# Row tiles 0 to 4 of an attention and feed-forward kernel in a written-out order

## The chip, the cores and the metric

The kernel runs on one core of one Trainium2 chip. The metric is device microseconds (us) of one launch. The kernel before takes 547.33 us, the median of 3 runs (546.87 to 547.88). TensorE (PE) multiplies, VectorE (DVE), ScalarE (ACT) and GpSimd (POOL) work on vectors, and SyncE (SP) issues nearly all DMA transfers.

## The reference

For eight batches of 512 rows of 512 numbers the kernel computes a cross attention against a context of 77 rows per batch, adds it to its input, and then a feed-forward layer with fake-quantised activations and weights, which is added too:

```python
q = layernorm(x) @ Wq                    # 8 heads of 64
k, v = context @ Wk, context @ Wv        # context: 8 x 77 x 384
attn = softmax(q @ k.T / 8)
x = x + (attn @ v) @ Wo + bo
xq = fake_quant(layernorm(x), clip_x)    # one scale for the whole tensor
h = silu(xq @ quant(w_gate).T) * (xq @ quant(w_up).T)     # 1408 wide
x = x + fake_quant(h, clip_down) @ quant(w_down).T
```

The two scales of `fake_quant` need the maximum over all rows, so the kernel has three stages: attention (about 20 to 300 us of the span), the gate and up products (to about 430 us), the down product. The change lies in the first.

## The kernel before

**Tiling.** The 4096 rows are 32 row tiles of 128 rows, n = 0 to 31; a batch b is four of them, and t = n % 4 is the place of a tile in its batch. Products that need full accuracy are made of three float32r products each, of high and low halves: the high half is an ACT copy (`split_hi`, `qo_hi`, `PT_high`), the low half a DVE or POOL subtraction (`split_lo`, `qo_lo`, `PT_low`).

**The steps of a row tile**, in the kernel's names:
- `q_chunk(b, m)`: 12 matmuls make a quarter of the queries of a batch in a QO bank; ACT copies it to `qs`. It needs all eight halves of the transposed input, `xTs`. `q(b,m)` for short.
- `S(n)`: 4 matmuls of scores into SP. `soft_max` and `soft_sub` (DVE) read SP and so free it for S(n+1). `soft_exp` (ACT), `soft_sum` and `soft_rec` (DVE), `soft_norm` (POOL, two instructions into `PN`) follow.
- `PT(n)`: 5 transposes into PTP; `PT_high` (ACT) and `PT_low` (DVE) take it to `pts`.
- `PV_rest(b)` and `PV(b, j)`, once a batch: attention times values, 24 matmuls into four banks; `qo_hi` (ACT) and `qo_lo` (DVE) take each to `os`. The values come back from DRAM by `load_vb(b)`, 12 small DMAs into `vbd`.
- `wo(n)`: 12 matmuls, then `residual` (DVE) adds the input with the bias, which `first_bias(n)` (POOL) had added. `first_stats`, `second_stats` and the like are the layer norms.
- `v_rows(r)`, r = 0 to 4: 9 matmuls make 128 rows of values for all batches; ACT and DVE halve them in `vst` (two slots), and SP stores them.
- Beside this, the feed-forward weights are turned to integers, 26 tiles i: `w_load` (SP), `w_top`, `w_scale`, `w_inverse` (DVE), `w_round` (ACT), `w_integer` (POOL and a store on SP). 22 of the tiles are 512 wide, and 4, rows of `w_down`, 1408 wide; `W_ORDER` says which is which.

**What sets the order.** There is no scheduler. Each call of `add` or `dma` appends an instruction to the queue of its engine, with semaphore waits; each engine runs its queue strictly in that order. So the order of the calls in the text is the order on every engine, SP's DMA queue among them. `attend(s)` is the written schedule of one step: it holds the weight tile s-1, the scores of tile s+1, the transposes of tile s, the output product of tile s-5, and so on, at places that depend on t. The steps 0 to 3 had exceptions of their own inside `attend` (`if s == 2` and the like), and `v_rows(0)` to `v_rows(4)` stood in between.

Of the kernel before, what the change touches and what calls it, by code (L numbers as in the profile page):

```python
# [62 lines left out]
def block_kernel(nc, x, xT, ctxT, Wq, Wk, Wv, Wo, bo, clip_x, clip_h, w_gate, w_up, w_down, out):  # L63
# [3 lines left out]
    NT, NI = 32, 11  # L67
# [6 lines left out]
    with ctx:  # L74
# [461 lines left out]
        def PV_rest(b):  # L536

            banks = []
            for j in range(2):
                at = state["use"] % 2  # L540
                state["use"] += 1
                banks.append((at, state["banks"][at], state["free"][at]))
            for k in range(2):
                banks.append((None, SP[:, 512 * k:512 * k + 512], (t_sub[min(4 * b + 4, NT - 1)],)))
            pv_at[b] = banks

            def fn(e):
                for i, (hv, hp) in enumerate(((0, 0), (0, 1), (1, 0))):
                    for j in range(4):
                        q = slice(32 * j, 32 * j + 32)  # L550
                        m = e.matmul(banks[j][1], vbd[q, hv, 4, :], pts[q, hp, 4, :], start=(i == 0), stop=False)
                return m
            add("pe", fn, [t_pl[4 * b + 3], t_vb[b], *(t for bank in banks for t in bank[2])], "qo_mm")

        def PV(b, j):
# [12 lines left out]
            if j < 2:  # L568
                state["free"][at] = (t_oss[b, j],)
# [86 lines left out]
        for at, tile in ((4, 22), (8, 23), (12, 24), (16, 25)):  # L656
            W_ORDER.insert(at, tile)
# [59 lines left out]
        t_pz = add("pool", lambda e: e.memset(PN[:, :, 512:640], 0.0), [t_ctxl, t_wkl], "c_pz")  # L717
        for k in range(4):
            split_hi(1, k)
            split_lo(1, k, ("dve", "pool")[k % 2])  # L720
        v_rows(0)
        S(0)
        soft_max(0)
        soft_sub(0)
        soft_exp(0)
        soft_sum(0)
        soft_rec(0)
        soft_norm(0)
        v_rows(1)
        S(1)  # L730
        soft_max(1)
        soft_sub(1)
        v_rows(2)
        soft_exp(1)
        for n in range(4, XR):
            load_xn(n, [])
        t_sge = add("act", lambda e: e.activation(sge[:, :], clips[:, :], ACT.Exp, scale=-1.0),
                    [t_clip], "sg_e")
        t_sg = add("dve", lambda e: e.tensor_scalar_add(sgp[:, :], sge[:, :], 1.0), [t_sge], "sg_p")
        t_sg = add("dve", lambda e: e.reciprocal(sg[:, :], sgp[:, :]), [t_sg], "sg")  # L740

        DEFER = (1, 2)

        def attend(s):
# [3 lines left out]
                  "pv": t == 0 and b >= 1}  # L748
# [14 lines left out]
            if s < 26 and s != 2:  # L763
# [3 lines left out]
            late_low = s - 1 >= 0 and (s - 1) % 4 in DEFER  # L767
            if t == 0:
# [33 lines left out]
            elif t < 3:  # L802
                if t == 1 and b + 1 < NB and s != 1:
                    q_chunk(b + 1, t)
# [12 lines left out]
                if b + 1 < NB:  # L817
                    if t == 2 or s == 1:
                        q_chunk(b + 1, t)
                    if t == 2:  # L820
                        q_chunk(b + 1, 3)
                if s == 2:
                    PT(s)
                    split_hi(2, 0)
                    split_hi(2, 1)
                    PT_high(s)
                    split_hi(2, 2)
                    split_hi(2, 3)
                    first_stats(5)
                    first_aggr(5)  # L830
                    PT_low(s)
                    split_lo(2, 2, "dve")
                    split_lo(2, 3, "dve")
# [17 lines left out]
            else:  # L851
                when("s", S, s + 1)
                when("s", soft_max, s + 1)
                if s > 3:
                    PT_low(s - 1)
                else:
                    v_rows(4)
                    PT(s)
                    PT_high(s)
# [12 lines left out]
                if s == 3:  # L872
                    q_chunk(2, 0)
# [14 lines left out]
            if s == 0:  # L888
                v_rows(3)
            if s == 1:  # L890
                for n in range(3):
                    first_bias(n)
# [534 lines left out]
```

How the kernel before makes its waits and increments, by code:

```python
    def run(self, engine, e):  # L47
        for need, fn, sem, by in self.queue[engine]:
            for s, v in need:
                e.wait_ge(s, v)
            ins = fn(e)
            if sem is not None:
                ins.then_inc(sem, by)
```

## Time and profile before

| | us |
|---|---|
| median of 3 runs | 547.33 |
| the profiled execution | 547.3 |
| its span | 545.5 |
| PE busy in the span | 528.1 (97%) |
| DVE busy | 475.3 (87%) |
| ACT busy | 294.2 (54%) |
| POOL busy | 231.8 (42%) |

The granted clock of PE is full throughout. Of the chain of work that ended last, PE holds 73% and DVE 12%. Matmuls are pipelined: one of 512 columns is shown 0.39 us long, and the next starts 0.23 us after it. So lengths of work on PE are best read from start to start.

### The profile page before, as it was taken

What the parts mean: (1) busy time and instruction counts of PE and PEld (TensorE: products, weight loads), DVE (VectorE), ACT (ScalarE), POOL (GpSimd) and SP (SyncE); (2) the same over time, 40 slices, a digit from 0 to 9 for tenths busy, and PEclk for the clock granted to TensorE, in tenths of its full rate; (3) what the DMA queues carried; (4) which work ended last, traced back from release to release, by engine and by line L of the source; (5) the groups of instructions that cost most, each with busy time, mean ns of one, the idle gap of its engine ahead of it and who ended that gap; (6) DMA issues with size and microseconds to landing.
All of it is one profiled execution on the core that took longest, in us unless ns stands there. A gap on an engine that the chain in (4) does not pass through costs nothing.

```text
span 545.5 us, 8102 instructions
## 1 busy us (share of the span) xinstructions
PE 528.1 (97%) x2740; PEld 355.9 (65%) x2740; DVE 475.3 (87%) x879; ACT 294.2 (54%) x414; POOL 231.8 (42%) x349
## 2 busy tenths in 40 slices
PE   8989889999999999999999899999999999999997
PEld 7868678787888878888788644444444445544444
DVE  4966988999989899898989799999999988899884
ACT  4834645556465654554534646555545533999500
POOL 4385858769596895856553000000000000055442
PEclk9999999999999999999999999999999999999999
DMA  8809375765668465545949955850442220399987
GB/s 315 275 41 301 92 210 171 226 215 160 214 212 272 143 216 178 178 129 165 203 88 313 282 122 242 283 141 22 116 117 44 72 38 5 123 328 234 159 106 127
DMA packets 82943, 93.83 MB, mean 172 GB/s; under 512 B 47085, under 2 KB 50157, under 8 KB 82645
## 3 DMA queue, kind: packets, MB, share of 16 engines
q1 hardware_dynamic: 77877, 84.13, 49.9%
q0 software_dynamic: 4320, 7.87, 9.6%
q10 hardware_dynamic: 704, 1.31, 0.7%
q8 instruction: 22, 0.36, 0.3%
q14 instruction: 20, 0.16, 0.1%
HBM read 47.51 MB, written 37.78 MB: 156 GB/s over the span
## 4 chain that ended last, share of the span: by engine, by line
PE 73%; DVE 12%; SPq 6%; DMA 3%; issue 2%; ACT 1%; POOL 1%; ACTq 0%; DVEq 0%; POOLq 0%
PE SP L1137 13%; PE QO L1137 13%; PE QO L192 5%; PE QO L194 4%; PE QO L193 4%; SPq L37 4%; PE SP L463 4%; PE QO L1294 4%; PE PTP L1294 3%; PE SP L1294 3%; SPq L41 2%; PE MI L583 2%; PE MI L582 2%; PE MI L581 2%; PE WOP L1294 2%
## 5 line engine op out<-in xcount | busy, mean ns | idle before, releaser
L45 POOL DMA_DIRECT2D out<-n2b x30 | 30.3, 1045 | 207.4 <-DVE n2b L1327 207.4
L1144 ACT ACTIVATE sil<-QO,fsc 128x512 f32<-128x512 f32 x87 | 59.8, 687 | 70.9 <-PE QO L1137 69.3
L1137 PE MATMUL SP<-nT,wgu 128*128 128x512 bf16 x340 | 87.3, 379 | 0.4
L1137 PE MATMUL QO<-nT,wgu 128*128 128x512 bf16 x340 | 87.3, 379 | 0.1
L1148 DVE SCALAR_TENSOR_TENSOR h<-SP,fsc,sil 128x512 f32<-128x512 f32 x87 | 65.1, 748 | 8.7 <-PE SP L1137 7.1
L504 POOL TENSOR_TENSOR PN<-P,rs 128x512 f32<-128x512 f32 x64 | 44.3, 714 | 50.2 <-DVE rs L496 50.2
L1151 DVE TENSOR_REDUCE hmx<-h 128x1 f32<-128x512 f32 x87 | 59.7, 686 | 3.0
L487 ACT ACTIVATE P<-P,r 128x616 f32<-128x616 f32 x32 | 26.0, 812 | 63.7 <-DVE P L483 63.7
L1137 PEld LDWEIGHTS SP<-nT,wgu 128*128 128x128 bf16 x340 | 32.9, 98 | 41.4 <-DVE h L1148 2.5
L1137 PEld LDWEIGHTS QO<-nT,wgu 128*128 128x128 bf16 x340 | 33.2, 98 | 40.2 <-ACT sil L1144 0.3
L192 PE MATMUL QO<-xTs,wqs 128*128 128x512 f32 x124 | 50.4, 407 | 2.3 <-DVE xTs L223 2.0
L1261 ACT ACTIVATE h<-h,magic,g 128x1536 f32<-128x1536 f32 (+2 forms) x38 | 47.8, 1350 | 3.3 <-DVE g L1073 3.3
L194 PE MATMUL QO<-xTs,wqs 128*128 128x512 f32 x124 | 48.5, 391 | 0.0
L193 PE MATMUL QO<-xTs,wqs 128*128 128x512 f32 x124 | 48.3, 390 | 0.0
L463 PE MATMUL SP<-kst,qs 128*128 128x154 f32 x248 | 38.1, 296 | 4.0 <-DVE P L483 1.8
L602 POOL TENSOR_TENSOR xn<-xn,bob 128x512 f32<-128x512 f32 x32 | 41.3, 1294 | 0.0
L686 ACT ACTIVATE wraw<-wraw,magic,wiv 128x512 f32<-128x512 f32 (+1 forms) x26 | 24.1, 928 | 31.2 <-DVE wiv L679 31.2
L463 PEld LDWEIGHTS SP<-kst,qs 128*128 128x128 f32 x248 | 34.5, 190 | 5.9 <-DVE P L483 2.2
L631 ACT ACTIVATE n<-x,mr,r 128x512 f32<-128x512 f32 x31 | 25.0, 808 | 15.5 <-POOL mr L625 15.5
L1264 DVE TENSOR_SCALAR wgu<-h 128x1536 bf16<-128x1536 f32 (+2 forms) x39 | 29.3, 757 | 1.2 <-ACT h L1261 0.7
L192 PEld LDWEIGHTS QO<-xTs,wqs 128*128 128x128 f32 x124 | 23.3, 188 | 7.8 <-issue 2.2
L493 DVE TENSOR_REDUCE sm<-P 128x8 f32<-128x616 f32 x32 | 25.1, 785 | 2.6 <-ACT P L487 1.7
(224 smaller groups left out, 1203.3 us busy)
## 6 DMA issues: line engine op xcount, KB each, us to landing
xTr<-in_xT SPq DMA_DIRECT2D x8, 1024.0 KB, 7.9
xn<-in_x SPq DMA_DIRECT2D x32, 256.0 KB, 3.8
out<-x SPq DMA_DIRECT2D x32, 256.0 KB, 2.9
n_rows<-n SPq DMA_DIRECT2D x32, 256.0 KB, 2.7
n2b<-n_rows SPq DMA_DIRECT2D x32, 256.0 KB, 3.8
out<-n2b POOLq DMA_DIRECT2D x30, 256.0 KB, 6.5
h_spill<-h SPq DMA_DIRECT2D x2, 2816.0 KB, 9.3
h<-h_spill SPq DMA_DIRECT2D x6, 768.0 KB, 7.2
```

The costliest lines, as they stand in the source:

```text
L192: e.matmul(ps, lh, rh, start=(i == 0), stop=False)
L193: e.matmul(ps, lh, rl, start=False, stop=False)
L194: m = e.matmul(ps, ll, rh, start=False, stop=(i == n - 1))
L463: m = e.matmul(o, qs[:, b % 2, j, w], kst[:, b, j, :], start=(j % 2 == 0), stop=True, skip_group_check=True)
L504: t_norm[n] = add("pool", lambda e, to=to, rb=rb, l0=l0, l1=l1: e.tensor_tensor(to, u[:, :, l0:l1], rb, ALU.mult), [t_rec[n], t_PT.get(n - ...
L602: t_xb[n] = add("pool", lambda e: e.tensor_tensor(xn[:, n % XR, :], xn[:, n % XR, :], bob[:, :], ALU.add), [t_bn1[n], t_bo], "xb")
L1137: m = e.matmul(ps, wv_[:, k, col:col + 128], nT[:, b % 2, :, k, :], start=(k == 0), stop=(k == 3))
L1144: t_sil[n] = add("act", lambda e: e.activation(sil[:, n % SR, :], gp, ACT.Silu, scale=fsc[:, ic:ic + 1]), [t_g[n], t_fs, t_h.get(n - SR)], ...
L1148: t_h[n] = add("dve", lambda e: e.scalar_tensor_tensor(out=hv, in0=up, scalar=fsc[:, 11 + ic:12 + ic], in1=sil[:, n % SR, :], op0=ALU.mult ...
L1151: t_hm[n] = add("dve", lambda e: e.tensor_reduce(hmx[:, n:n + 1], hv, AX.X, ALU.max, apply_absolute_value=True), [t_h[n]], "hmx")
L1261: a = add("act", lambda e: e.activation(hv, hv, ACT.Identity, bias=magic[:, :], scale=g2[:, 1, 1:2]), [t_g2] + ([t_back[b, p]] if b < 2 el ...
L1294: mm = e.matmul(ps, hq[:, i % 2, k, tt * 128:tt * 128 + 128], wd[:, k, :], start=(k == 0), stop=(k == NI - 1))
```

## The change

It touches the order alone; every instruction that computes is still there.

- Row tiles 0 to 4 are no longer made by `attend(0)` to `attend(3)` but by a list of calls ahead of the loop, and the loop begins with `attend(4)`. At that point the same steps have been done as before, and in addition `PV_rest(0)` and `PV(0, 0..3)`, which stood in `attend(4)`.
- `v_rows` is cut in two: `v_mm(r)` (the matmuls) and `v_out(r)` (the halves and the store). S(0) comes directly behind q(0,3), and the value rows come behind scores.
- `PV_rest(0)` uses the banks MI and WOP for its pairs 0 and 1 and QO for 2 and 3, in place of QO and SP; so S(5) waits for no copy of it.
- The loads of `xn` and of weight tiles 0 and 1 stand ahead of the stores of the value rows.
- The wide tiles move from the places 4, 8, 12, 16 of `W_ORDER` to 9, 13, 17, 21. A tile at place i is converted in step i+1: so from steps with t = 1 to steps with t = 2.

```diff
-        def v_rows(r):
+        def v_mm(r):
...
+            v_at[r] = qo_bank(pairs, 512, m, [t_wvl, t_ctxl])
+
+        def v_out(r):
...
+            th = add("act", lambda e: e.activation(hi, bank, ACT.Copy), [t, t_v.get(r - 2)], "qo_hi")
...
+            t_v[r] = dma("sp", vd[r * 128:r * 128 + m], vst[0:m, r % 2], [th, tl], f"st_v{r % 2}")
...
-            if t == 1 and b > 0:
+            if t == 1 and b > 1:
                 free += [t_oss[b - 1, 2], t_oss[b - 1, 3]]
...
-            banks = []
+            banks = [] if b else [(None, MI[:, :], ()), (None, WOP[:, :], (t_c,))]
...
-        for at, tile in ((4, 22), (8, 23), (12, 24), (16, 25)):
+        for at, tile in ((9, 22), (13, 23), (17, 24), (21, 25)):
...
+        S(0)
+        v_mm(0)
+        soft(0, "max", "sub", "exp")
+        v_out(0)
+        v_mm(1)
+        S(1)
+        soft(0, "sum", "rec", "norm")
+        soft(1, "max", "sub")
+        v_out(1)
+        load_vb(0)
+        v_mm(2)
+        soft(1, "exp")
+        S(2)
+        split_lo(1, 0, "dve")
+        soft(1, "sum", "rec", "norm")
+        first_bias(0)
+        soft(2, "max", "sub")
+        v_out(2)
+        split_lo(1, 2, "dve")
+        t_xT[2] = load_xT(2, t_xTs[1])
+        v_mm(3)
+        soft(2, "exp")
+        PT(0)
+        PT_high(0)
+        v_out(3)
+        q_chunk(1, 0)
...
+        q_chunk(1, 3)
...
+        S(4)
+        soft(4, "max", "sub")
+        PV_rest(0)
+        PV(0, 2)
+        soft(4, "exp")
+        split_hi(2, 3)
+        split_lo(2, 2, "dve")
+        PV(0, 3)
+        soft(4, "sum", "rec", "norm")
+        split_lo(2, 3, "dve")
+        PV(0, 0)
+        PV(0, 1)
+        q_chunk(2, 0)
+        first_bias(4)
+        w_tops(2)
+        w_round(2)
+        w_integer(2)
...
-        for s in range(28):
+        for s in range(4, 28):
             attend(s)
```

**DVE, between the scores of tile 4 and the query chunk q(2,0).** `xTs` is a low half of the input of batch 2, `mx`, `P`, `sm`, `rs` are the softmax, `pts` is `PT_low`, `vst` the last value rows. Before:

```order
L223 TENSOR_TENSOR pts<-PTP,pts 128x5x128
L223 TENSOR_TENSOR xTs<-xTr,xTs 128x512 x2
L476 TENSOR_REDUCE mx<-SP 128x8
L211 TENSOR_TENSOR vst<-QO,vst 104x512
L483 TENSOR_TENSOR P<-SP,mx 128x616
```

Now, where `os` is the low half of a pair of attention times values:

```order
L486 TENSOR_REDUCE mx<-SP 128x8
L493 TENSOR_TENSOR P<-SP,mx 128x616
L577 TENSOR_TENSOR os<-QO,os 128x512
L223 TENSOR_TENSOR xTs<-xTr,xTs 128x512
L577 TENSOR_TENSOR os<-QO,os 128x512
L503 TENSOR_REDUCE sm<-P 128x8
L506 RECIPROCAL rs<-sm 128x8
L223 TENSOR_TENSOR xTs<-xTr,xTs 128x512
L577 TENSOR_TENSOR os<-MI,os 128x512
L577 TENSOR_TENSOR os<-WOP,os 128x512
```

The two low halves that q(2,0) waits for stood ahead of the scores of tile 4; now the second stands behind two `os` halves and the sum of tile 4.

**ACT, at the same place.** `qs` is the copy of a query chunk, `wraw` is `w_round`. Before, the chunk is q(2,0), and the rounding is that of weight tiles 2 and 3:

```order
L219 ACTIVATE qs<-QO 128x512
L686 ACTIVATE wraw<-wraw,magic,wiv 128x512 x2
L565 ACTIVATE os<-SP 128x512 x2
L565 ACTIVATE os<-QO 128x512 x2
L219 ACTIVATE pts<-PTP 128x5x128
```

Now (the first `qs` after the `os` copies is q(2,0)):

```order
L576 ACTIVATE os<-QO 128x512
L497 ACTIVATE P<-P,r 128x616
L219 ACTIVATE xTs<-xTr 128x512
L576 ACTIVATE os<-QO 128x512
L576 ACTIVATE os<-MI 128x512
L576 ACTIVATE os<-WOP 128x512
L219 ACTIVATE qs<-QO 128x512
L697 ACTIVATE wraw<-wraw,magic,wiv 128x512 x2
```

The rounding of weight tiles 2 and 3 stood ahead of the four `os` copies and now stands behind them and behind the chunk q(2,0), which comes after all of PV(0).

**SP, the DMA queue, from the second load of transposed input on.** `v_halves` are stores of value rows, `vbd` the 12 loads of `load_vb(0)`. Before:

```order
L37 DMA xTr<-in_xT 128x4x512
L37 DMA v_halves<-vst 128x1024 x3
L37 DMA xn<-in_x 128x512 x5
L37 DMA wraw<-in_ffn_w_gate 128x512
L37 DMA xTr<-in_xT 128x4x512
L37 DMA v_halves<-vst 128x1024
L37 DMA wraw<-in_ffn_w_gate 128x512
L37 DMA wgu_ints<-wint 128x512
L37 DMA wraw<-in_ffn_w_gate 128x512
L37 DMA vbd<-v_halves 64x4x64 x4
L37 DMA vbd<-v_halves 13x2x64 x8
```

Now:

```order
L37 DMA xTr<-in_xT 128x4x512
L37 DMA xn<-in_x 128x512 x5
L37 DMA wraw<-in_ffn_w_gate 128x512 x2
L37 DMA v_halves<-vst 128x1024 x2
L37 DMA vbd<-v_halves 64x4x64 x4
L37 DMA vbd<-v_halves 13x2x64 x8
L37 DMA v_halves<-vst 128x1024
L37 DMA xTr<-in_xT 128x4x512
L37 DMA v_halves<-vst 128x1024
```

Loads went ahead of the stores, and `load_vb(0)` ahead of the third store of value rows. For batch 1 the row of SP is the same as before: store of weight tile 2, load of tile 4, `xTr`, 12 `vbd`, store of tile 3, load of tile 5.

## Rows read from the trace of the kernel before

**Rows 1.** Busy time of each engine in two stretches; count of instructions in brackets.

```profile
core 0: us, PE busy (x) PEld busy (x) DVE busy (x) ACT busy (x) POOL busy (x), PEclk, DMA share, GB/s
30.30:73.60 43.30, 37.34 (x195) 29.84 (x193) 33.18 (x60) 21.86 (x38) 32.14 (x37) 1.00 0.53 165
...
96.30:300.00 203.70, 202.30 (x1078) 167.45 (x1079) 186.73 (x373) 109.08 (x167) 139.13 (x238) 1.00 0.64 195
```

**Rows 2.** What PE waited for, 30 to 80 us: total, times, longest.

```profile
PE SP L463 <- DVE P L483: 1.8, 1, 1.8
PE SP L463 <- DVE os L566: 1.6, 1, 1.6
PE QO L192 <- DVE xTs L223: 1.1, 1, 1.1
PE QO L551 <- DMA vbd<-v_halves: 0.9, 1, 0.9
PE SP L463 <- ACT qs L219: 0.6, 1, 0.6
```

**Rows 3.** Timeline of PE: start us, length us, instruction, [idle before].

```profile
30.33 0.39 PE L192 MATMUL QO<-wvs,cts 128*128 128x512 f32 x1
...
46.37 1.21 PE L463 MATMUL SP<-kst,qs 128*128 128x154 f32 x8
47.31 0.49 PE L192 MATMUL QO<-xTs,wqs 128*128 128x512 f32 x1
...
50.18 0.71 PE L516 MATMUL PTP<-identF,PN 128*128 128x128 f32 x5
50.73 1.22 PE L463 MATMUL SP<-kst,qs 128*128 128x154 f32 x8
...
67.61 0.50 PE L551 MATMUL QO<-pts,vbd 32*128 32x512 f32 x2 [0.90 <-DMA vbd<-v_halves]
...
68.51 0.50 PE L559 MATMUL SP<-pts,vbd 128*128 128x512 f32 x1
...
71.38 0.71 PE L516 MATMUL PTP<-identF,PN 128*128 128x128 f32 x5
73.64 1.29 PE L463 MATMUL SP<-kst,qs 128*128 128x154 f32 x8 [1.55 <-DVE os L566]
...
96.29 0.47 PE L192 MATMUL QO<-xTs,wqs 128*128 128x512 f32 x1
```

**Rows 4.** Timeline of POOL and DVE, 31.5 to 34 us.

```profile
29.47 4.61 POOL L223 TENSOR_TENSOR wos<-wor,wos 128x2048 fp32r<-128x2048 f32 x1
...
31.68 2.95 DVE L223 TENSOR_TENSOR xTs<-xTr,xTs 128x512 fp32r<-128x512 f32 x1 [3.35 <-ACT xTs L219]
```

**Rows 5.** The chain that ended last, 30 to 38 us: start, us, what.

```profile
34.55 0.68 DVE xTs L223
```

**Rows 6.** Timeline of ACT and DVE, three instructions.

```profile
30.53 0.60 ACT L219 ACTIVATE qs<-QO 128x512 f32<-128x512 f32 x1 [2.12 <-PE QO L194]
...
47.62 0.80 DVE L476 TENSOR_REDUCE mx<-SP 128x8 f32<-128x616 f32 x1 [1.76 <-PE SP L463]
48.45 0.80 DVE L483 TENSOR_TENSOR P<-SP,mx 128x616 f32<-128x616 f32 x1
```

**Rows 7.** Stores of value rows: time from issue to landing.

```profile
DMA to landing us min/median/max: 2.6/5.8/9.0
```

**Rows 8.** Timeline of SP, 69 to 83 us.

```profile
70.06 0.37 SPq L37 DMA_DIRECT2D wgu_ints<-wint  x1
...
71.62 9.82 SPq L37 DMA_DIRECT2D vbd<-v_halves  x12
...
82.04 0.42 SPq L37 DMA_DIRECT2D wraw<-in_ffn_w_gate  x1
```

**Rows 9.** DMA issues, 60 to 120 us: count, KB each, median us to landing.

```profile
wraw<-in_ffn_w_gate SPq DMA_DIRECT2D x6, 256.0 KB, 2.9
```

**Rows 10.** Timeline of DVE and ACT in step 6.

```profile
86.97 0.67 DVE L670 TENSOR_REDUCE wmx<-wraw 128x1 f32<-128x512 f32 x1
...
91.87 0.69 ACT L219 ACTIVATE pts<-PTP 128x640 fp32r<-128x640 f32 x1
```

More of the change, by code:

```diff
@@ L542, in PV_rest @@
                 banks.append((at, state["banks"][at], state["free"][at]))
-            for k in range(2):
-                banks.append((None, SP[:, 512 * k:512 * k + 512], (t_sub[min(4 * b + 4, NT - 1)],)))
+            if b:
+                for k in range(2):
+                    banks.append((None, SP[:, 512 * k:512 * k + 512], (t_sub[min(4 * b + 4, NT - 1)],)))
             pv_at[b] = banks
@@ L567, in PV @@
                               [th, *waits], "qo_lo")
-            if j < 2:
+            if at is not None:
                 state["free"][at] = (t_oss[b, j],)
@@ L717, in block_kernel, with soft, row_stats, w_tops @@
         t_pz = add("pool", lambda e: e.memset(PN[:, :, 512:640], 0.0), [t_ctxl, t_wkl], "c_pz")
+        def soft(n, *steps):
+            for step in steps:
+                {"max": soft_max, "sub": soft_sub, "exp": soft_exp, "sum": soft_sum, "rec": soft_rec,
+                 "norm": soft_norm}[step](n)
+        def row_stats(n):
+            first_stats(n)
+            first_aggr(n)
+            first_scale(n)
+        def w_tops(i):
+            w_top(i)
+            w_scale(i)
+            w_inverse(i)
         for k in range(4):
             split_hi(1, k)
[L720 to L734, printed above, removed]
+        split_lo(1, 1)
+        split_lo(1, 3)
         for n in range(4, XR):
             load_xn(n, [])
+        w_load(0)
+        w_load(1)
+        S(0)
[24 more added lines that the diff above has]
+        q_chunk(1, 0)
+        soft(2, "sum", "rec", "norm")
+        first_bias(1)
+        PT_low(0)
+        S(3)
+        row_stats(3)
+        soft(3, "max", "sub")
+        PT(1)
+        PT_high(1)
+        soft(3, "exp")
+        q_chunk(1, 1)
+        PT_low(1)
+        soft(3, "sum", "rec", "norm")
+        first_bias(2)
+        first_bias(3)
         t_sge = add("act", lambda e: e.activation(sge[:, :], clips[:, :], ACT.Exp, scale=-1.0),
@@ L740, in block_kernel @@
         t_sg = add("dve", lambda e: e.reciprocal(sg[:, :], sgp[:, :]), [t_sg], "sg")
+        w_tops(0)
+        v_mm(4)
+        w_round(0)
+        w_integer(0)
+        v_out(4)
+        t_flat = [t_v[4], t_v[3], t_wol, ("qo_mm", c.count["qo_mm"])]
+        PT(2)
+        PT_high(2)
+        w_load(2)
+        q_chunk(1, 2)
+        PT_low(2)
+        row_stats(4)
+        PT(3)
+        PT_high(3)
+        w_tops(1)
+        w_round(1)
+        w_integer(1)
+        w_load(3)
+        q_chunk(1, 3)
+        PT_low(3)
+        row_stats(5)
+        for k in range(3):
+            split_hi(2, k)
+        split_lo(2, 0)
+        split_lo(2, 1)
+        S(4)
[15 more added lines that the diff above has]
+        w_integer(2)
+        row_stats(6)
+        first_bias(5)
+        first_bias(6)
         DEFER = (1, 2)
@@ L761, in turned @@
                 PT_high(s)
-            if s < 26 and s != 2:
+            if s < 26:
                 w_load(s)
@@ L802, in attend @@
             elif t < 3:
[L803 removed]
+                if t == 1 and b + 1 < NB:
                     q_chunk(b + 1, t)
@@ L816, in attend @@
                 when("w", w_inverse, s - 1)
[L817 to L833, printed above, removed]
+                if b + 1 < NB and t == 2:
+                    q_chunk(b + 1, 2)
+                    q_chunk(b + 1, 3)
                 when("w", w_round, s - 1)
@@ L853, in attend @@
                 when("s", soft_max, s + 1)
[L854 to L859, printed above, removed]
+                PT_low(s - 1)
                 when("s", soft_sub, s + 1)
-                if s == 3:
-                    PT_low(s)
                 when("s", soft_exp, s + 1)
-                if s > 3 and b + 2 < NB:
+                if b + 2 < NB:
                     split_lo(b + 2, 3, "dve")
@@ L887, in attend @@
                 when("n2", normed, s - 6)
[L888 to L892, printed above, removed]
             when("s", soft_norm, s + 1)
@@ L895, in attend @@
             if more:
-                for k in range(2 if s == 2 else 3):
+                for k in range(3):
                     split_lo(b + 2, k)
```

58 lines of the change are left out of this document (22 added, 36 removed).

## The prediction, made before the changed kernel ran

> **What bounds the kernel now.** I read first the busy time by stretch. From 96 us to the end of attention PE is busy 202.30 of 203.70 us [rows 1]: there PE sets the pace, and the change moves no matmul of that stretch. From 30.3 to 73.6 us PE is busy 37.34 of 43.30 us, so 6.0 us are idle [rows 1]. The list of PE's waits names all of them: S(1) behind a late subtraction (1.8), S(5) behind a copy of PV(0) (1.6), q(2,0) behind a low half (1.1), PV_rest(0) behind the last `vbd` load (0.9), S(4) behind its query copy (0.6) [rows 2]. The timeline then gives lengths from start to start: S 0.94 us (46.37 to 47.31), a query chunk behind it 2.87 (to 50.18), PT 0.55 (to 50.73), PV_rest 0.90 (67.61 to 68.51), PV 2.87 (to 71.38) [rows 3]. A block of values is 9 matmuls of 0.23, 2.1 us, and 0.1 more behind scores.
>
> The change removes no work. It is worth what it takes from the 6.0 us, less what it puts in their place, and less what is lost again before 96.29 us, the start of q(3,0) [rows 3]. From there on the order is the old one but for the wide tiles. So I replay the new order by hand from 30.33 us, where q(0,3) has been issued.
>
> **Part 1: tiles 0 to 4, step by step.**
>
> (a) S(0) directly behind q(0,3). It waits for the query copy, which runs 30.53 to 31.13 [rows 6]; before, value rows started at 30.33 and hid it [rows 3]. S(0) starts at 31.16: 0.8 us of new idle.
>
> (b) S(0), values 0 and 1, S(1), values 2, S(2), values 3: 3 x 0.94 + 4 x 2.1 + 3 x 0.1 = 11.5, to 42.7. Do the scores wait? A max starts 1.25 us behind its scores, the subtraction 0.83 later, and takes 0.80 [rows 3, 6]: 2.9 us in all. For S(0) that is 34.1, and S(1) is due at 36.4; for S(1) 39.3, and S(2) is due at 39.6. No wait; the 1.8 us of rows 2 goes. It had come from DVE standing in a low half of `xTs` for 2.95 us [rows 4], whose own length is 0.68 [rows 5]; that op is now behind the scores.
>
> (c) PT(0) to 43.3, then q(1,0), which waits for the low half (1,2). DVE has ahead of it the low half of value rows 1, half (1,0), sum and reciprocal of tile 1, max and subtraction of tile 2 (to 43.05) and value rows 2 (to 43.6). Alone the half would end at 44.3. But `first_bias(0)` stands on POOL from 42.9 to 44.2, and in rows 4 the same DVE op, started at 31.68 beside a POOL op that ended at 34.08, ended only at 34.63, 0.55 us behind it. So I let it end 0.55 behind the bias, at 44.7, and q(1,0) start at 44.8: 1.5 us idle. Bounds: 1.0 if the two don't meet; 2.1 if the DVE op also meets the next POOL op.
>
> The Trainium skill, page "SBUF — State Buffer", section "SBUF: two separate sides", says that VectorE with two SBUF inputs and GpSimd hold a port pair in turn, each for its whole instruction. By that rule, the trace agrees (34.08 and 34.63); a sum without it would come out 0.4 us lower.
>
> (d) q(1,0), S(3), PT(1), q(1,1), values 4, PT(2), q(1,2), PT(3), q(1,3): 4 x 2.85 + 0.94 + 3 x 0.55 + 2.1 = 16.1, to 60.9. Softmaxes, PT_low and the halves of value rows are done 0.3 us or more ahead of each.
>
> (e) S(4) directly behind q(1,3) waits for its query copy: 0.8 us (0.6 before, rows 2). S(4) at 61.7.
>
> (f) S(4), PV_rest(0), PV(0): 1.05 + 0.90 + 2.87, to 66.55, without a wait, since `vbd` is issued 40.4 to 50 now. The 0.9 goes. Then q(2,0) waits for low half (2,3), which now stands behind PV's copies. The subtraction of tile 4 ends at 61.7 + 3.0 = 64.7. ACT: `os` high of pair 2 to 65.25, exp (0.7 from start to start) to 65.95, `split_hi(2,3)` to 66.5, `os` high of pair 3 to 67.05. DVE: `os` low 0.6, sum 0.83, reciprocal 0.12, half (2,3) 0.68: 69.3. q(2,0) starts at T = 69.3: 2.8 us idle where 1.1 stood. This is the largest new wait. Bounds 2.0 to 3.7: pair 2 and exp overlap less or more by one op of 0.8.
>
> (g) q(2,0) 2.8, PT(4) 0.55: S(5) at T + 3.35 = 72.65, with no wait for PV's copies. Before it was 73.64 [rows 3]. So here the kernel is 1.0 us ahead.
>
> **Part 2: what is given back.** w_round(2) stands on ACT behind the copy of q(2,0). That copy ends at T + 3.6, the rounding at T + 4.5, `w_integer(2)` on POOL (0.6) at T + 5.1. SP is in order: store of tile 2, load 4, `xTr`, then 12 `vbd` issues of 9.82 us together, store of tile 3, load of tile 5. From that store to load 5 SP took 70.06 to 82.04, 12.0 us [rows 8]. So load 5 is issued at T + 17.1 = 86.4, and lands 2.9 later [rows 9]: L = 89.3. Queued behind it on DVE is all that follows `w_top(5)`, which before ran at 86.97 [rows 10] and 1 us ahead would be due at 86.0. DVE had 2.3 us of slack at its next wait for PE; the rest is late. Sum 7, the scale, w_round(5), four `split_hi` and PT_high(6) follow one another: from `w_top(5)` to the end of PT_high(6) rows 10 show 5.6 us, of which 0.4 was a wait for exp, so 5.2. Then PT_low(6) 0.8, subtraction 0.7, low half (3,3) 0.7 and 0.1: q(3,0) at L + 7.6 = 96.9. Before it was at 96.29 [rows 3]. The 1.0 us gained has become 0.6 us lost. Bounds of this part: nothing given back (load in time), or 1.3 more if the load takes 4.2 us behind the `vbd` packets.
>
> **Part 3: wide tiles at t = 2.** DVE has 1.0 us more in steps 10, 14, 18, 22 and 1.0 less in the step before. Both lie ahead of the same DVE wait for the output product, so that DVE arrives there at the same time. ACT and POOL get 0.7 more each, ahead of `split_hi` and behind the low halves. I take 0; bounds -0.5 to +1.0, a quarter of a us for each of the four.
>
> **Part 4: the rest.** `PV_rest(0)` in other banks, the split of `v_rows` and the clip constants cost nothing on PE; the same number of matmuls is issued. The early loads of `xn` and of tiles 0 and 1 take away two DVE waits that PE did not share.
>
> **Sum.** Against the profiled execution, 547.3 us (span 545.5): + 0.6 = 547.9. The median of the runs, 547.33, differs from it by less than 0.1 us, so the sum stands for both. As (c) and (f) may as well be shorter by half an op, I put 547.8.
>
> **Rivals.**
> 1. *The gain stays (load 5 hidden).* If SP's issues run faster or w_round(2) is sooner, L is at 86 or less, and the 1.0 us of (g) goes to the end: 546.3; with (f) at its low bound 545.5. For it: PE is full from 96 us on, so nothing else takes it. Against it: L must come 3 us sooner, and the 12.0 us of SP repeat the same DMAs. Chance 0.26.
> 2. *The old waits simply go.* S(0), q(1,0), S(4) and q(2,0) find their inputs ready and 5 of the 6 us are won: 542 to 544. Against it: steps (a) and (e) are waits for a copy behind its own matmuls, and no order hides them here. Chance 0.05.
> 3. *The store of value rows holds ACT.* `v_out(4)` waits on ACT for the store of value rows 2, because they share a slot of `vst`, and that store is now behind the 12 `vbd` issues: issued at 50.0. ACT needs it at 55.1; behind `v_out(4)` are PT_high(2), the copy of q(1,2) and PT_high(3), and PT(3) on PE waits for PT_low(2). Landings were 2.6 to 9.0 us [rows 7]. It decides from a landing of 5.1 us; at the median 5.8 it costs under 1, at 9.0 it costs 3.5: then T is later by as much: 548.5 to 551.3. Against it: the 9.0 was behind 2 MB of other loads, and now nearly nothing is ahead. Chance 0.12.
> 4. *Low half (2,3) later still, or wide tiles costly*: the upper bounds of (f) or part 3, 548.5 to 549.5. Chance 0.17.
> 5. Forecast: 547.8, own range 547.0 to 548.5. Chance 0.40.
>
> A difference of 0.2% is 1.1 us, about what a measurement tells from no change: 546.2 and 548.4 are the limits. Rival 2 and most of rival 1 are faster, with a little of the forecast's lower side: 0.29. Rivals 3 and 4 and a little of the forecast are slower: 0.30. The rest, 0.41, is the same. The range is 545.7 to 549.6: below it lie rival 2 and the extreme of rival 1, above it the long landings of rival 3.
>
> **What would show it.** In the profile of the changed kernel: the wait of S(1) gone; S(0) waiting 0.7 to 0.8 for `qs`; q(1,0) waiting 1 to 2 for `xTs`; PE idle 2.0 to 3.7 us ahead of q(2,0), waiting for DVE `xTs`; S(5) near 72.7; DVE `w_top` (wmx) waiting near 86 us about 3 us for the DMA of `wraw`; q(3,0) near 96.9. The prediction is wrong if DVE doesn't wait for that load, if ACT waits for a store ahead of a `vst` copy, or if PE shows new idle time after 100 us.

## The result, and the profile of the changed kernel

The changed kernel takes 560.31 us, the median of 3 runs (559.49 to 563.32), against 547.33: a ratio of 1.0249, with a 95% interval of 1.0214 to 1.0284. It is 13 us slower, and the time forecast, 547.8 with a range up to 549.6, was wrong.

The profiled execution took 563.32 us (span 561.5). The busy times in the two stretches, as in [rows 1]:

```profile
30.30:73.60 43.30, 37.70 (x188) 30.26 (x188) 31.82 (x58) 20.00 (x34) 26.90 (x30) 0.96 0.39 121
96.30:300.00 203.70, 190.80 (x1008) 155.87 (x1007) 176.06 (x350) 102.55 (x154) 136.98 (x226) 0.99 0.59 178
```

The part that was replayed step by step shows about the same busy time, at a mean granted clock of 0.96, so with a little less work in it. Most of the loss is in the other stretch, where PE was busy 202.30 us and is now busy 190.80. The profiled execution is the slowest of the three; 2.0 us of its loss lie ahead of q(3,0), the rest behind.

**Tiles 0 to 4.** PE's waits from 30 to 80 us, which answer to [rows 2]: total, times, longest.

```profile
PE QO L192 <- DVE xTs L223: 4.1, 2, 2.7
PE SP L473 <- ACT qs L219: 1.4, 2, 0.7
PE PTP L526 <- DVE pts L223: 0.2, 1, 0.2
```

The same on PE's timeline: S(0), q(1,0), S(4), q(2,0), its fifth matmul, S(5), and q(3,0), which answers to the last line of [rows 3].

```profile
31.10 1.32 PE L473 MATMUL SP<-kst,qs 128*128 128x154 f32 x8 [0.69 <-ACT qs L219]
44.84 0.47 PE L192 MATMUL QO<-xTs,wqs 128*128 128x512 f32 x1 [1.41 <-DVE xTs L223]
61.89 1.32 PE L473 MATMUL SP<-kst,qs 128*128 128x154 f32 x8 [0.69 <-ACT qs L219]
69.70 0.64 PE L192 MATMUL QO<-xTs,wqs 128*128 128x512 f32 x1 [2.66 <-DVE xTs L223]
71.43 0.63 PE L193 MATMUL QO<-xTs,wqs 128*128 128x512 f32 x1
74.67 1.22 PE L473 MATMUL SP<-kst,qs 128*128 128x154 f32 x8
98.32 0.47 PE L192 MATMUL QO<-xTs,wqs 128*128 128x512 f32 x1 [0.67 <-DVE xTs L223]
```

Steps (a) to (f) came within 0.4 us of the forecast. Behind the 2.66 us of idle the matmuls are 0.63 us long and 0.43 apart, where they were 0.39 and 0.23: the granted clock is 0.67 of full in 70 to 75 us, about 1.6 us lost. In the profile of the first experiment the same wait (2.63) has no such stretch behind it.

DVE's low half (1,2) beside POOL's bias addition, as in [rows 4]:

```profile
42.87 1.27 POOL L613 TENSOR_TENSOR xn<-xn,bob 128x512 f32<-128x512 f32 x1
43.48 1.21 DVE L223 TENSOR_TENSOR xTs<-xTr,xTs 128x512 fp32r<-128x512 f32 x1
```

POOL ends at 44.14 and DVE at 44.69, again 0.55 us behind.

**The load of weight tile 5** (step 6 takes it), as in [rows 8, 10]: the 12 `vbd` issues, the load behind them on SP, and `w_top(5)`.

```profile
77.75 9.33 SPq L37 DMA_DIRECT2D vbd<-v_halves  x12
...
87.68 0.42 SPq L37 DMA_DIRECT2D wraw<-in_ffn_w_gate  x1
```

```profile
90.74 0.69 DVE L681 TENSOR_REDUCE wmx<-wraw 128x1 f32<-128x512 f32 x1 [3.28 <-DMA wraw<-in_ffn_w_gate]
```

**The rest of the attention.** PE's waits from 80 to 315 us, then the longest of DVE's. Before, the same list for PE has 0.9 for `xTs` and 0.3 for `pts` in this stage.

```profile
PE PTP L526 <- DVE pts L223: 5.1, 4, 1.7
PE SP L473 <- DVE os L577: 4.2, 4, 1.2
PE QO L192 <- DVE xTs L223: 3.2, 5, 0.7
PE QO L562 <- DVE pts L223: 0.3, 1, 0.3
```

```profile
DVE pts L223 <- ACT pts L219: 6.6, 6, 1.6
DVE wmx L681 <- DMA wraw<-in_ffn_w_down: 6.5, 4, 2.2
DVE bn L599 <- DMA xn<-in_x: 5.3, 5, 1.6
```

That is 12.8 us on PE. One wait of each kind stands ahead of the first wide tile and belongs to the late tile 5 and the late row of SP behind it (0.36 ahead of PT(7), 0.67 ahead of q(3,0), 0.49 ahead of S(9)), and the last line is the same as before. The other 11.0 us follow the four wide tiles: 0.63 to 0.67 for `xTs` behind each of them, 1.3 to 1.75 for `pts` behind three (not the third), 1.2 for `os` behind three (not the first, where the clock had fallen). Read back from PE in batch 2, this is **chain 1**: load of the wide tile on SP, `w_top`, `w_round`, four `split_hi`, `PT_high(10)`, `PT_low(10)`, PT(11), q(4,0).

```profile
118.89 0.42 SPq L37 DMA_DIRECT2D wraw<-in_ffn_w_down  x1
```

```profile
124.77 1.62 DVE L681 TENSOR_REDUCE wmx<-wraw 128x1 f32<-128x1408 f32 x1 [2.17 <-DMA wraw<-in_ffn_w_down]
...
131.67 0.82 DVE L223 TENSOR_TENSOR pts<-PTP,pts 128x640 fp32r<-128x640 f32 x1 [1.56 <-ACT pts L219]
```

```profile
127.40 1.57 ACT L697 ACTIVATE wraw<-wraw,magic,wiv 128x1408 f32<-128x1408 f32 x1 [2.93 <-DVE wiv L690]
128.87 2.17 ACT L219 ACTIVATE xTs<-xTr 128x512 fp32r<-128x512 f32 x4
130.95 0.68 ACT L219 ACTIVATE pts<-PTP 128x640 fp32r<-128x640 f32 x1
```

```profile
132.64 0.74 PE L526 MATMUL PTP<-identF,PN 128*128 128x128 f32 x5 [1.75 <-DVE pts L223]
134.01 0.47 PE L192 MATMUL QO<-xTs,wqs 128*128 128x512 f32 x1 [0.63 <-DVE xTs L223]
```

The load was issued at 118.89, behind the 12 `vbd` issues and one store. In the kernel before, the wide load went 3.9 us ahead of them:

```profile
101.98 0.44 SPq L37 DMA_DIRECT2D wraw<-in_ffn_w_down  x1
...
105.88 9.66 SPq L37 DMA_DIRECT2D vbd<-v_halves  x12
```

DVE's first read takes 1.62 us (a tile 512 wide takes 0.67), ACT's rounding 1.57 (0.82).

**Chain 2** leads to the scores of the second tile of the next batch, behind batch 3 to S(17). It starts at the same `w_round`, for which the `split_hi` and so POOL's low halves wait. In batch 3 POOL has no gap from 166.10 to 178.38: three low halves, the wide integer op, the norms, the softmax, the next weight tile's integer op, and `mr` (row norm). ACT's `normed` waits for it, the rounding of the next tile and the `os` copies stand behind, and PE waits for DVE's `os`.

```profile
169.94 1.69 POOL L703 TENSOR_SCALAR wint<-wraw 128x1408 bf16<-128x1408 f32 x1
...
178.11 0.27 POOL L636 TENSOR_SCALAR mr<-mv,r 128x1 f32<-128x1 f32 x1
```

```profile
178.41 0.82 ACT L642 ACTIVATE n<-x,mr,r 128x512 f32<-128x512 f32 x1 [2.56 <-POOL mr L636]
179.13 0.80 ACT L697 ACTIVATE wraw<-wraw,magic,wiv 128x512 f32<-128x512 f32 x1
179.83 1.06 ACT L576 ACTIVATE os<-SP 128x512 fp32r<-128x512 f32 x2
```

```profile
181.88 1.29 PE L473 MATMUL SP<-kst,qs 128*128 128x154 f32 x8 [1.24 <-DVE os L577]
```

This run of POOL is not new. Before, it went without a gap from 156.51 to 168.09 us, 11.6 us in place of 12.3, and `normed` waited for its end too, but only 1.13 us, and PE did not wait:

```profile
168.12 0.82 ACT L631 ACTIVATE n<-x,mr,r 128x512 f32<-128x512 f32 x1 [1.13 <-POOL mr L625]
```

### The profile page after: what moved, and what is told of

Its sections match the earlier page's. It is cut to its first block, busy times and chain, and to the rows that moved or that the text cites. A ratio compares the mean times of both kernels' runs of the same rounds, so it can differ in the third digit from the quotient of the medians.

```text
span 561.5 us, 8093 instructions
## 1 busy us (share of the span) xinstructions
PE 532.4 (95%) x2733; PEld 357.4 (64%) x2740; DVE 474.0 (84%) x879; ACT 293.6 (52%) x414; POOL 231.3 (41%) x349
## 4 chain that ended last, share of the span: by engine, by line
PE 55%; DVE 11%; SPq 10%; POOL 8%; DMA 6%; issue 5%; ACT 3%; ACTq 0%; DVEq 0%; POOLq 0%
PE SP L1194 13%; PE QO L1194 12%; SPq L37 10%; DMA wraw<-in_ffn_w_down 4%; PE PTP L1351 3%; PE QO L1351 3%; PE SP L1351 3%; POOL xTs L223 3%; PE QO L192 2%; PE QO L193 2%; PE QO L194 2%; PE SP L473 2%; PE WOP L1351 2%; POOL wint L703 2%; DMA wkr<-in_xattn_Wk 1%
## 5 line engine op out<-in xcount | busy, mean ns | idle before, releaser
L192 PE MATMUL QO<-xTs,wqs 128*128 128x512 f32 x124 | 51.9, 418 | 7.3 <-DVE xTs L223 7.3
L193 PE MATMUL QO<-xTs,wqs 128*128 128x512 f32 x124 | 49.6, 400 | 0.0
L194 PE MATMUL QO<-xTs,wqs 128*128 128x512 f32 x124 | 49.6, 400 | 0.0
L486 DVE TENSOR_REDUCE mx<-SP 128x8 f32<-128x616 f32 x31 | 24.5, 789 | 10.6 <-PE SP L473 10.4
L223 DVE TENSOR_TENSOR pts<-PTP,pts 128x640 fp32r<-128x640 f32 x31 | 25.2, 813 | 6.1 <-ACT pts L219 6.1
```

Source lines behind the costliest of these rows:

```text
L192: e.matmul(ps, lh, rh, start=(i == 0), stop=False)
L193: e.matmul(ps, lh, rl, start=False, stop=False)
L194: m = e.matmul(ps, ll, rh, start=False, stop=(i == n - 1))
```

## The experiments

Each has 3 rounds; a ratio is to the kernel before on the same chip. "Waits" are PE's in the attention from 80 us on; the kernel before has 1.2. The runs f3 to f7 stand in their own parts below.

| | median us | ratio, 95% | waits |
|---|---|---|---|
| changed kernel | 560.31 | 1.0214 to 1.0284 | 12.8 |
| e1 wide tiles at the old places | 549.86 | 1.0026 to 1.0059 | 3.4 |
| e2 only the wide tiles moved | 558.44 | 1.0160 to 1.0229 | 10.6 |
| e3 old phase, one batch later | 549.85 | 1.0019 to 1.0053 | 3.1 |
| e4 wide tiles at t = 3 | 557.99 | 1.0153 to 1.0217 | 9.2 |
| f1 load cut | 558.36 | 1.0184 to 1.0230 | 9.0 |
| f2 conversion cut | 553.81 | 1.0093 to 1.0134 | 5.3 |
| g1 store later | 561.63 | 1.0212 to 1.0266 | 11.6 |
| g2 load cut, store later | 557.94 | 1.0141 to 1.0209 | 9.3 |
| h1 store later, norm behind `os` | 568.91 | 1.0351 to 1.0425 | 14.4 |
| h2 norm behind `os` | 567.19 | 1.0319 to 1.0410 | 14.0 |
| h3 load cut, store later, norm behind `os` | 558.37 | 1.0154 to 1.0234 | 8.5 |
| i1 store and norm later | 561.88 | 1.0233 to 1.0304 | 10.8 |
| i2 load cut, store and norm later | 553.74 | 1.0075 to 1.0147 | 5.7 |

### Is it the written-out part or the wide tiles?

```diff
 e1_old_places: the changed kernel with
+        for at, tile in ((4, 22), (8, 23), (12, 24), (16, 25)):
 e2_before_new_places: the kernel before with
+        for at, tile in ((9, 22), (13, 23), (17, 24), (21, 25)):
 e3_later_same_phase and e4_one_step_on: the changed kernel with
+        ((8, 22), (12, 23), (16, 24), (20, 25))
+        ((10, 22), (14, 23), (18, 24), (22, 25))
```

> The changed kernel, wide weight tiles back at places 4, 8, 12, 16. Theory P (the wide tile's load at places 9, 13, 17, 21 is issued on SP behind the 12 vbd loads and lands late, 11 of the 13 us): 547.5 to 549.5 us, no DVE wait for a w_down load, PE idle from 100 to 300 us about 1 us. Rival O (the written-out order of tiles 0 to 4 costs most of the 13 us): 556 to 560. The wait of DVE for weight tile 5 (3.3 us near 87 us in the changed kernel) stays under both.

> The kernel before, with nothing changed but the wide tiles at places 9, 13, 17, 21. Theory P: 556 to 559 us, and PE waits 1.2 to 1.8 us for pts and 0.6 for xTs once in each of four batches. Rival O: 547 to 548.5.

> The changed kernel, wide tiles at places 8, 12, 16, 20: four steps later than before, but loaded in a step with t = 0, ahead of the vbd loads. Theory P: same as with the old places within 1 us, 547.5 to 549.5. Rival L (later as such is what costs, as rows, stores and weights pile up): 553 to 560.

> The changed kernel, wide tiles at places 10, 14, 18, 22: loaded in a step with t = 2, not behind the vbd loads, converted in a step with t = 3. Theory P: 548 to 552, DVE waits under 0.5 us for a w_down load. Rival W (the length of the wide tile on DVE, ACT and POOL, 1.0, 0.75 and 0.75 us more, is what a step other than t = 1 can't hold, whenever it lands): 556 to 562, as at 9, 13, 17, 21 or worse.

The wide tiles cost 10.4 us in the new order (560.31 to 549.86) and 10.9 in the old one (558.44 to 547.59 in that call). So two things are left to explain: these 10.5 us, and the 2.3 us by which e1 is slower than before. That e3 equals e1 says that the phase in the batch decides, not which batch. At t = 3 there is no DVE wait for the load, yet the cost is 8.1 us, through another row:

```profile
PE QO L562 <- ACT qs L219: 6.2, 4, 1.6
```

Here the wide rounding stands on ACT ahead of the copy of q(b+2,0), and PV_rest waits for its bank. So length alone is enough to cost time, where it falls on a chain without slack. This is the rival's time (556 to 562); the theory that the late load is all had asked for 548 to 552.

### Load or length?

```diff
 f1_wide_load_cut: in w_load
+            n = 4 if i > 9 else n
 f2_wide_narrow_conv: in w_top, w_round and w_integer
+            v = wraw[:, i % 2, 0:(n if i < 10 else 4) * 128]
```

> The changed kernel (wide tiles at 9, 13, 17, 21); the last three of the four wide tiles load only 512 of their 1408 columns, and are still converted over all 1408. Left out: the other columns of the load. Theory P (late landing of the wide load): three of four losses of about 2.7 us shrink to under 0.7 us: 551 to 554 us. Rival W (the length of the conversion): 558 to 560.5, as the changed kernel.

> The changed kernel; the wide tiles are loaded in full, but the last three are converted (maximum, rounding, integers) over 512 columns only. Left out: the rest of their conversion. Theory P alone: 558 to 560. Rival W alone: 551 to 553. Both, one behind the other on the same chain (landing, maximum, rounding, split_hi, PT_high, PT_low): 554 to 557, as 1.0 us of DVE and 0.75 of ACT go in each of three batches.

For the three tiles that were cut, the length gives 6.5 us (f2: 553.81, just under the 554 to 557 expected if load and length both cost). The load gives 2.0: f1 is within the rival's times, and its interval overlaps that of the changed kernel, so this run alone doesn't tell the gain from nothing. f2 shortens the op on DVE, ACT and POOL at once; no run says which of the three counts most. In f1, PE's waits for `pts` and `xTs` fell to 1.0 and 2.3 us, but the one for `os` rose from 4.2 to 5.4. Chain 1 was relieved and chain 2 took over.

### What carries the wait for os?

My first theory for chain 2 was SP's order: its store of the wide tile waits for POOL and stands ahead of the load of `xn`, for which DVE waits 5.3 us.

```diff
 g1_store_behind_out, g2_cut_and_store_behind (with f1's cut): in step t = 3
-            if s < 26:
+            if s < 26 and not later:
                 w_load(s)
...
                 x_in()
+                if later:
+                    held.pop()()        # store of the wide tile
+                    w_load(s)
```

> The changed kernel, with SP's order altered around the wide tiles: the store of a wide tile and the load behind it, which both wait for POOL's long integer op, now stand behind the store of the rows x and the load of xn of the same step, not ahead of them. Nothing else is changed. Theory of two chains: the wait S(4b+1) <- DVE os (4.2 us in 4 in the changed kernel) comes only through this store (POOL integer late, SP held, xn load late, DVE bn late), so it goes, and the first chain (wide load late, DVE and ACT late, PT and q late, 8.3 us) stays: 555.0 to 557.5, with the DVE wait for xn near 1 us in all and PE's wait for os under 1. Rival (one chain: all lateness is that of the load and of the longer vector work, SP's order only changes its name): 559 to 561, the os wait is replaced by a longer wait of PT or q.

> The same order on SP, and the last three of the four wide tiles are loaded only 512 columns wide, though converted over all 1408 columns (the other 896 columns of these tiles hold old data, so the output of the down product is not that of the reference). With the load cut alone the kernel took 558.36, and its largest PE wait was os (5.4 us in 5). Theory of two chains: with both cut, what is left of the 10.5 us is the longer DVE and ACT work itself: 552.0 to 554.5; os wait under 1.5 us. Rival: the length of the conversion is all, 557 to 558.5.

That theory fell. DVE's wait for `xn` is gone in g1, and PE's wait for `os` is still 4.2 us in 4; g2 came to its rival's time. Batch 3 of g1 shows why:

```profile
177.24 0.82 ACT L642 ACTIVATE n<-x,mr,r 128x512 f32<-128x512 f32 x1 [2.59 <-POOL mr L636]
```

```profile
180.71 1.29 PE L473 MATMUL SP<-kst,qs 128*128 128x154 f32 x8 [1.25 <-DVE os L577]
```

From the wide integer op (168.74) to the scores it is 11.97 us, in the changed kernel 11.94 (169.94 to 181.88). By these rows the chain runs over POOL and ACT, and the wait for `xn` had stood beside it. So `normed`, which waits for POOL, was put behind the `os` copies.

```diff
 h1_norm_behind_os (g1 with it), h2_norm_behind_os_only, h3_all_three_cut (g2 with it): in t == 0
-                when("n2", normed, s - 6)
...
                         PV(b - 1, j)
+                when("n2", normed, s - 6)
```

> The kernel with the wide store behind the row store (561.63), and in the steps with t = 0 the norm of tile s-6 on ACT, which waits for POOL's mr, stands behind the four os copies and not ahead of them. POOL theory (POOL is busy without a gap from 164.9 to 177.2 us, wide integer among it; ACT's norm waits 2.6 us for its mr, and the os copies stand behind the norm): the wait S(4b+1) <- DVE os, 1.2 us in each of 4 batches, goes: 556.0 to 558.0, ACT's wait for mr ahead of os gone, PE's wait for os under 1.5 us in all. Rival (the os copies are late through w_round or PE itself): 560 to 562, os wait as before.

> The changed kernel with that move of the norm alone; SP's order is as in the changed kernel, so the load of xn stands behind the wide store, and DVE's statistics, the scale and w_round of the next weight tile wait for it (wiv ends at 178.64 us, mr at 178.38). If POOL's chain and SP's chain end together in front of the os copies, as these two ends say: 558.5 to 560.5, at most 0.4 us a batch gained, os wait 0.8 to 1.1 each. If POOL's alone decides and SP's is harmless: 555.5 to 557.5. If neither matters: 560 to 562.

> Load of the last three wide tiles cut to 512 columns (the rest of these tiles is old data, as before), the wide store behind the row store, and the norm behind the os copies; the conversion is at its full length. With the first two alone it was 557.94, with an os wait of 5.4 us in 5. POOL theory: 552.0 to 553.5, os wait under 1.5 us; what is left above 549.9 is the longer DVE and ACT work ahead of PT and q (xTs, pts waits 3 to 4 us) and the wait of the first wide tile, which is loaded in full. Rival: 556.5 to 558.

Measured were 568.91 us (ratio 1.0351 to 1.0425), 567.19 (1.0319 to 1.0410) and 558.37 (1.0154 to 1.0234). PE's wait for `os` went as expected (none in h1), but the totals did not follow; h1 and h2 are slower than either of their forecasts, and h3 is 0.4 above its rival's. `normed` also issues a store. It now stood on SP ahead of the `vbd` issues and waited for ACT; in g1 they had begun at 179.87:

```profile
182.89 0.33 SPq L37 DMA_DIRECT2D n_rows<-n  x1
183.31 9.31 SPq L37 DMA_DIRECT2D vbd<-v_halves  x12
...
193.23 0.42 SPq L37 DMA_DIRECT2D wraw<-in_ffn_w_down  x1
```

The wide load was 2.9 us later than in g1 (193.23 to 190.29), and PE waited 11.0 us for `pts` in place of 3.8. In each of the four batches the clock fell behind that wait; batch 4:

```profile
206.16 0.74 PE L526 MATMUL PTP<-identF,PN 128*128 128x128 f32 x5 [2.34 <-DVE pts L223]
207.52 0.47 PE L192 MATMUL QO<-xTs,wqs 128*128 128x512 f32 x1 [0.63 <-DVE xTs L223]
...
208.74 0.63 PE L193 MATMUL QO<-xTs,wqs 128*128 128x512 f32 x1
```

I had made the mistake of part 3 again: of a moved step every instruction counts, its DMA too. h1 and h2 therefore don't test the POOL theory. The last pair puts it right.

```diff
 i1_norm_behind_vbd (in place of h1), i2_cut_norm_behind_vbd (h3):
                 load_vb(b)
+                when("n2", normed, s - 6)
                 PT_high(s)
```

> The kernel with the wide store behind the row store (561.63); in the steps with t = 0 the norm of tile s-6 stands on ACT behind the four os copies, and its store on SP behind the 12 vbd issues. POOL theory, now without the side effect on SP: the os wait (4.2 us in 4) goes and the vbd issues start no later than before (1.2 us earlier a batch, as PE does): 556.5 to 558.0, os under 1 us, DVE's wait for the wide load 4 to 7 us in all. Rival (the load on SP is bound by its own row of issues, so the wide load comes no earlier and its wait takes over the 1.2 us of each batch): 560.5 to 562, with pts and xTs waits of 10 to 12 us.

> The same with the load of the last three wide tiles cut to 512 columns (the rest of these tiles is old data), compared with 557.94 with the norm ahead of the os copies, where PE waited 5.4 us for os. POOL theory: 552.0 to 553.5, os wait under 1 us; with the load late by only 0 to 0.5 us nothing else takes its place. Rival: 556 to 558.

With the load in full, the move of the norm gives nothing (561.63 to 561.88, the rival's value). With the load cut it gives 4.2 us (557.94 to 553.74; 0.2 above the expected span). In i1, and then in i2, PE waited:

```profile
PE PTP L526 <- DVE pts L223: 7.3, 4, 2.6
PE QO L192 <- DVE xTs L223: 3.2, 5, 0.7
```

```profile
PE QO L192 <- DVE xTs L223: 2.6, 5, 0.7
PE SP L473 <- DVE os L577: 1.7, 1, 1.7
...
PE PTP L526 <- DVE pts L223: 1.1, 3, 0.5
```

In i1 PE's wait for `os` is gone (4.2 in g1), and the one for `pts` has grown from 3.8 to 7.3, as has DVE's wait for the wide load (5.3 to 9.0). So the two chains hold each batch side by side. Four runs with the store later show it: cutting the load alone gives 3.7 us (g1 to g2), moving the norm alone nothing (g1 to i1), both together 7.9 (g1 to i2), of the 10.5 that the wide tiles cost.

i2 is still 3.9 us above e1. The 1.7 for `os` in it stands ahead of S(9) at 110.14, before any wide tile is loaded: it is the late `xn` of part 2 (e1 waits 0.95 there). Behind the wide tiles i2 has 2.8 us of waits, 2.1 of them at the first, which is loaded in full, and the last. The rest stays open.

### The 2.3 us of the written-out part

```diff
 f4_low_halves_early (e1 with it): ahead of S(4)
+        for k in (2, 3, 0, 1):
             split_hi(2, k)
+        split_lo(2, 2, "dve")
+        split_lo(2, 3, "dve")
 f5_tile2_early (e1 with it): ahead of S(4), in place of behind q(2,0)
+        w_tops(2)
+        w_round(2)
+        w_integer(2)
 f6_tile2_and_low_halves: both. f7_low_half_12_early: f6 and
         split_lo(1, 0, "dve")
+        split_lo(1, 2, "dve")
...
-        soft(2, "max", "sub")
+        soft(2, "max")
         v_out(2)
-        split_lo(1, 2, "dve")
+        soft(2, "sub")
```

> The changed order of tiles 0 to 4 with the wide tiles at the old places (549.9), and the high halves 2 and 3 and the low halves 2 and 3 of batch 2's input ahead of S(4) instead of behind PV's copies. Step (f) of the prediction: q(2,0) starts at 67, not 69.7, with PE idle under 0.3 us before it, the weight chain starts 2.7 us sooner too: 546.8 to 547.8. Rival (the loss of 2.3 us lies in the weight and vbd chain alone, DVE is as late as before in batch 1): 549 to 550.

> As the changed order with wide tiles at the old places (549.9), but maximum, rounding and integers of weight tile 2 ahead of S(4) instead of behind q(2,0). Part 2 of the prediction: SP stores tile 2, loads tile 4 and starts the 12 vbd issues about 5 to 8 us sooner; DVE no longer waits for the load of tile 5; q(2,0) stays at 69.7 and q(3,0) comes at 95.7 to 96: 547.5 to 548.5. Rival (the loss is all PE idle up to S(5)): 549.5 to 550.

> The changed kernel with the wide tiles at their old places, and with both repairs of the handwritten part: the low halves of batch 2 ahead of S(4), and the conversion of weight tile 2 ahead of S(4). Alone they gave 547.35 and 547.31, against 549.86 without either. If the two waits (PE's 2.7 us ahead of q(2,0), and the gate load that came late because tile 2 was converted late) are separate: 545.0 to 546.0, under the kernel before, q(3,0) near 93, no DVE wait for the gate load. If the gate load is late anyway once PE is 2.6 us earlier: 546.8 to 547.6.

> The handwritten part with both repairs and the wide tiles at their old places (545.66), and in addition the low half (1,2) directly behind (1,0), ahead of the softmax of tile 2, so that it runs before POOL's bias addition of tile 0, and the subtraction of tile 2 behind the value halves. If PE's wait ahead of q(1,0) (1.4 us) is that DVE op held to 0.55 us behind the POOL op: the wait falls under 0.6 and the time to 544.4 to 545.1. If the wait for the copy behind it or for the softmax takes its place: 545.4 to 546.2.

f4: 547.35 us (0.9986 to 1.0011); the wait of 2.7 ahead of q(2,0) is gone. f5: 547.31 (0.9988 to 1.0025); DVE no longer waits for the gate load, and q(3,0) starts at 95.64 in place of 97.15. f6: 545.66 (0.9937 to 0.9970), f7: 544.93 (0.9946 to 0.9976). Both beat the kernel before by 0.4 to 0.5%. In f7 the 1.4 us ahead of q(1,0) are gone, and 1.0 of them stands ahead of PT(1) instead, which waits for the `pts` of tile 0; f6 and f7 did not run side by side, so their order is open.

### The granted clock

```diff
 f3_dummy_matmuls (e1 with it): ahead of q(2,0)
+                m = e.matmul(PTP[:, 0:128], ones[:, :], ones[:, :], start=True, stop=True)   # 10 times
```

> The changed kernel with the wide tiles at their old places, and 10 matmuls of ones (128 columns) in the free PTP bank in the 2.7 us in which PE waits ahead of q(2,0). They end before the low half is there, so they cost nothing by themselves. If the idle time is what lets the granted clock fall in some runs (0.66 to 0.67 in 70 to 75 us in two of the profiles, 1.6 us): all runs within 0.8 us of each other, 549.3 to 549.9. If the clock falls for another cause: the spread of the runs stays 1.7 us or more (549.5 to 551.2 without the dummies), same median.

The 10 runs lay from 548.92 to 550.04, 1.1 us apart (e1: 549.47 to 551.15), median 549.29, ratio 1.0013 to 1.0038. The spread fell between the two forecasts. The clock of each run says more. With the 2.6 us of idle ahead of q(2,0) left as it is and the wide tiles at t = 1, 13 of 30 runs have a mean granted clock of 0.994 to 0.997 (4 of e1, 5 of e3, 4 of f5, 10 runs each), the others 0.999 or 1.0. With the gap filled (f3) or taken away (f4, f6, f7), all 35 runs have 0.999 or 1.0. So that idle time lets the clock fall, in some executions and not in others. It is not the only place: of the 19 runs of the kernel before that ran beside e1, 8 had 0.993 to 0.997 too, and no trace was kept of one.

## Why the prediction was wrong

**Part 1 held.** S(0) 31.10 (31.16 forecast), q(1,0) 44.84 (44.8), S(4) 61.89 (61.7), q(2,0) 69.70 (69.3) with 2.66 us of idle (2.8). DVE ended 0.55 us behind POOL again, as in [rows 4]. The Trainium skill, "SBUF — State Buffer", "SBUF: two separate sides", has a VectorE instruction with two SBUF inputs wait for a whole GpSimd instruction that reads SBUF; the trace agrees (44.14 and 44.69). S(5) was 2 us late against 72.65, of which 1.6 is the fallen clock. Rival 3 did not come: ACT's `vst` copy of value rows 4 ran at 55.53 without a wait.

**Part 2 had the right mechanism and too small a sum.** The load of tile 5 was issued at 87.68 (86.4), `w_top(5)` waited 3.28 us and ran at 90.74 (89.3). Without the fallen clock, in e1, q(3,0) started at 97.15 (96.9). The step gave 0.9 us lost against [rows 3], not 0.6. (The terms behind L add up to 7.5, not 7.6, so the sum should have said 0.5.) Behind it came what I had not followed: S(9) waits 0.95 us for `os`, because the same late row of SP had delayed an `xn` (DVE waits 1.7 us for it). Together that is most of the 2.3 us that e1 shows; f5, which takes away the late load alone, has neither wait.

**Part 3 is the step that failed.** "I take 0; bounds -0.5 to +1.0" measured 10.5 us. The sentence argued that the extra DVE time lies ahead of a DVE wait for PE. It does, but that wait was used up. From 80 us on, before and now:

```profile
DVE x L607 <- PE MI L583: 11.7, 6, 2.4
```

```profile
DVE x L618 <- PE MI L594: 3.4, 2, 2.4
```

Two things were left out.
- The load. I moved the conversion in thought, not its DMA. A tile that is converted at t = 2 is loaded in the step with t = 1, behind the 12 `vbd` issues of the step before, which [rows 8] shows to take 9.82 us, and DVE waits 6.5 us for it in 4 batches. I had used exactly this row in part 2.
- ACT and POOL. I wrote that they "get 0.7 more each", even named the place ahead of `split_hi`, and priced it at nothing without a reason. But ACT's rounding stands ahead of `split_hi` and `PT_high`, and POOL's integer op (1.69 us for 0.62) in a run of 12 us without a gap that ends in `mr`, ahead of ACT's `os` copies. f2, which takes away the length of three tiles, gives 6.5 us. Busy shares of 54% and 42% don't tell how much slack such a chain has.

Without part 3 the time is that of e1, 549.86: 2.1 us above the forecast and 0.3 above the range, since the small misses of part 2 all go one way. Rival 4 named costly wide tiles, but its price was the upper bound of part 3, so the range could not hold the time. The last condition, new idle time on PE after 100 us, is what came.

The rule of the Trainium skill, "DMA: Bandwidth & Descriptors", "Issuing engines are not separate DMA queues", says that the time to initiate a DMA is usually small beside the DMA. For one load of 256 KB the trace agrees: 0.42 us on SP, and 2.9 to its landing [rows 9]. But the 12 small loads together hold SP for 9.33 us, and what stands behind them waits that long before it is even issued.

## What to carry to other kernels

When work is moved to another step, replay it on every engine that it touches, and first of all its load on the DMA queue: ask what stands ahead of it there now. An engine at 42% can still be a chain without a gap for 12 us; read from the timeline what follows the lengthened instruction, up to the first wait that it could fill. Two chains that end in one batch hide each other, so an experiment that frees only one shows little or nothing (3.7 us and none here, 7.9 together), and the pair must be cut together.

## What the runs showed of the hardware

- The granted clock was 0.67 of full in 70 to 75 us, behind 2.66 us of idle PE, and 0.66 in 134 to 139 us, behind 1.75 and 0.63 us with a PT between: there matmuls of 512 columns are 0.43 us apart (the 1.2 GHz level), elsewhere 0.23. In batch 3 the same waits (1.71 and 0.63) left the clock at full. One such stretch costs about 1.6 us, and runs of one kernel differ by as much and more: i1's were 560.35 and 560.53 at a mean clock of 0.994, 563.24 and 564.15 at 0.988.
- Ten small matmuls in the idle 2.66 us (f3) kept the clock at 0.999 or more in 10 of 10 runs; without them it fell to 0.996 or 0.997 in 4 of 10 (e1).
- In h1 the wait for `pts` in each of four batches (2.3 to 2.8 us) lowered the clock every time: 0.95 on the mean in each of the four stretches of 36 us from 130 to 274 us. PE's waits grew by 2.8 us against g1, the median by 7.3. So a wait on PE can cost more than its own length.
